# Linear attention with a gated FFN on one Trainium2 core: the readout of the attention state on 32x32 tiles, with q moving

## What is computed

```python
xn = _layernorm(x, axis=-1)
q = jax.nn.elu(split_heads(xn @ Wq.T)) + 1.0
k = jax.nn.elu(split_heads(xn @ Wk.T)) + 1.0
v = split_heads(xn @ Wv.T)
kv_state = jnp.einsum('bhnd,bhne->bhde', k, v)
k_state = k.sum(axis=2)
attn_out = jnp.einsum('bhnd,bhde->bhne', q, kv_state)
denom = jnp.maximum(jnp.einsum('bhnd,bhd->bhn', q, k_state), 1e-06)[..., None]
attn_out = (attn_out / denom).transpose(0, 2, 1, 3).reshape(b, s, d)
local = xp[:, :-2, :] * conv_w[:, 0] + xp[:, 1:-1, :] * conv_w[:, 1] + xp[:, 2:, :] * conv_w[:, 2] + conv_b
attn = (attn_out + local) @ Wp.T + bp
ffn = (silu(xn @ wg.T) * (xn @ wu.T)) @ wd.T      # wg, wu, wd: int32 weights / 127, hidden size 768
out = x + attn + ffn
```

## Time and profile before

| what | us |
|---|---|
| median of 3 runs | 505.0 (504.65 to 505.31) |
| the profiled execution | 504.68 |
| its span, first to last instruction | 503.0 |
| TensorE busy in the span | 490.9 (98%) |
| VectorE busy | 429.3 (85%) |
| ScalarE busy | 332.9 (66%) |
| GpSimd busy | 145.8 (29%) |

### The profile page before, as it was taken

The page is one execution under the profiler, slowest core; times in us unless marked ns, Lnnn a source line. Parts: engine busy times, 40 slices in busy tenths (PEclk is TensorE's granted clock), DMA queues, the critical chain, the costliest instruction groups (busy, mean ns, idle before and its releaser), DMA issues.

```text
span 503.0 us, 11007 instructions
## 1 busy us (share of the span) xinstructions
PE 490.9 (98%) x3957; PEld 305.2 (61%) x3957; DVE 429.3 (85%) x827; ACT 332.9 (66%) x522; POOL 145.8 (29%) x162
## 2 busy tenths in 40 slices
PE   7989998999999999999999999999999999999997
PEld 6545364755657475574756657475565747657576
DVE  6797998889888888888889888889988889897787
ACT  1878857667485666748577585767748567674771
POOL 4476034140501414032140502314041141401050
PEclk9999999999999999999999999999999999999999
DMA  8637332343335324252342325233342432234012
GB/s 300 192 46 166 64 106 42 86 111 56 130 44 142 69 47 132 44 155 42 100 108 42 125 42 167 42 83 106 53 133 42 129 79 42 86 50 76 3 42 85
DMA packets 68669, 45.36 MB, mean 90 GB/s; under 512 B 33440, under 2 KB 68128, under 8 KB 68640
## 3 DMA queue, kind: packets, MB, share of 16 engines
q1 hardware_dynamic: 59232, 35.66, 25.5%
q0 software_dynamic: 8448, 8.39, 11.1%
q10 hardware_dynamic: 960, 0.92, 0.5%
HBM read 20.32 MB, written 8.39 MB: 57 GB/s over the span
## 4 chain that ended last, share of the span: by engine, by line
PE 86%; DVE 8%; ACT 3%; issue 2%; POOL 0%; DVEq 0%; POOLq 0%; ACTq 0%
PE ps L1126 16%; PE ps L1285 15%; PE ps L1304 15%; PE ps L1294 14%; PE ps L1228 14%; PE ps L1184 5%; PE ps L1193 3%; PE ps L1247 2%; DVE hid L975 1%; DVE hl L981 1%; PE ps L1134 1%; DVE local L904 1%; PE ps L1169 1%; ACT hh L590 1%; DVE p_wl L745 1%
## 5 line engine op out<-in xcount | busy, mean ns | idle before, releaser
L582 ACT ACTIVATE act_g<-ps,scales 128x512 f32<-128x512 f32 x96 | 66.0, 687 | 42.0 <-PE ps L1294 40.0
L975 DVE SCALAR_TENSOR_TENSOR hid<-act_g,scales,ps 128x512 f32<-128x512 f32 x96 | 71.4, 744 | 21.3 <-ACT act_g L582 20.7
L981 DVE TENSOR_TENSOR hl<-hid,hh 128x512 f16<-128x512 f32 x96 | 66.7, 694 | 2.2 <-ACT hh L590 0.8
L365 POOL TENSOR_TENSOR xT<-xh,xl 128x1024 f32<-128x1024 f16 x15 | 31.8, 2122 | 112.5 <-issue 98.1
L590 ACT ACTIVATE hh<-hid 128x512 f16<-128x512 f32 x96 | 59.7, 622 | 5.4 <-DVE hid L975 5.4
L1285 PE MATMUL ps<-xh,g_wh 128*128 128x512 f16 x192 | 57.6, 382 | 2.1 <-DVE q_relu L930 1.2
L1294 PE MATMUL ps<-xl,g_wh 128*128 128x512 f16 x192 | 57.1, 379 | 0.0
L1294 PE MATMUL ps<-xl,u_wh 128*128 128x512 f16 x192 | 57.1, 379 | 0.0
L1285 PE MATMUL ps<-xh,u_wh 128*128 128x512 f16 x192 | 57.1, 379 | 0.0
L1304 PE MATMUL ps<-d_wh,hh 128*128 128x256 f16 x384 | 52.5, 273 | 1.3 <-DVE hid L975 1.3
L330 POOL TENSOR_SCALAR xn<-x_in,neg_mean,rstd 128x256 f32<-128x256 f32 x62 | 52.3, 857 | 4.3 <-POOL rstd L337 4.2
(11 more groups left out here) (162 smaller groups left out, 964.7 us busy)
## 6 DMA issues: line engine op xcount, KB each, us to landing
xb<-bp_sb SPq DMA_DIRECT2D x16, 512.0 KB, 3.3
xb<-in_L_attn_x_dram POOLq DMA_DIRECT2D x16, 512.0 KB, 5.9
x_in<-in_L_attn_x_dram SPq DMA_DIRECT2D x15, 512.0 KB, 4.2
out_dram<-out_sb SPq DMA_DIRECT2D x14, 512.0 KB, 2.9
wg_int<-in_L_ffn_w_gate_dram SPq DMA_DIRECT2D x1, 768.0 KB, 6.9
wu_int<-in_L_ffn_w_up_dram SPq DMA_DIRECT2D x1, 768.0 KB, 8.4
wd_int<-in_L_ffn_w_down_dram SPq DMA_DIRECT2D x1, 768.0 KB, 11.2
out_dram<-out_sb SPq DMA_DIRECT2D x3, 256.0 KB, 2.1
```

Of the source, the lines that this page charges most:

```text
L582: nc.scalar.activation(act_g[:, j % 2, :], ps[:, gate_bank(j), :], ACT.Silu, scale=silu_in).then_inc(silu_ready, 1)
L975: nc.vector.scalar_tensor_tensor(out=hid[:, j % 2, :], in0=act_g[:, j % 2, :], scalar=h_mul, in1=ps[:, gate_bank(j) + 1, :], op0=ALU.mult, ...
L981: nc.vector.tensor_tensor(hl[:, j, :], hid[:, j % 2, :], hh[:, j, :], ALU.subtract).then_inc(hl_ready, 1)
```

## The change

The readout is done the other way round. The state stays **stationary** in its compact form and q moves, so the result has channels on its partitions at once and there is nothing to turn back.

- `denominators`: four matmuls per chunk, `key_sums` (128 x 32, of which 8 columns are not zero) stationary on the four 32-column strips, 256 tokens of q moving. One half of the channels and one half of the tokens for each strip.
- `divide_one`: maximum and reciprocal of the 128 x 256 denominators, once per chunk. Of the 128 rows 32 hold denominators.
- `spread_den`: four DMAs on SyncE's queue copy each of the 8 rows to the 16 partitions of its head, 128 x 256 fp32 (128 KB) each, to `over_den` in q's layout.
- `divide_q`: q is multiplied by it, 128 x 1024.
- `numerators`: eight matmuls per chunk, each with a 32x32 block of the compact state stationary and 512 tokens of q moving. Those of the first half of the channels stand on the diagonal of the array (row strip r, column strip r) and write bank 4 (6 or 2 in the last step), those of the second half on row strip r, column strip r-1, and write the next bank.
- For that, wq's second half is loaded turned by 32 channels (three DMAs in place of one), and the accumulation of the second half stands on strips turned by one.
- `state` needs no spreading; the mask is reduced once to 128 x 32. `normalise` and `transpose_attn` are gone.
- `put_y` moves behind `hidden_low(0)`, `put_q` behind `hidden_low(4)`. `accumulate(1)` moves behind `gate_up(0)`, the numerators behind `gate_up(1)`. The last step is put in a new order.

Between `den_inv` and `q_divided` now lie the four DMAs; the numerators wait for `q_divided`. On SyncE `spread_den` stands first in the step, ahead of the load of x.

The diff, cut to its core:

```diff
+            def spread_den(b, c):
+                sp.wait_ge(den_inv, at(b, c, 1, 1))
+                for k in range(KT):
+                    for h in range(2):
+                        rows = slice((2 * k + h) * GROUP, (2 * k + h) * GROUP + HPB)
+                        sp.dma_start(over_den[:, c, k, h * DEN_TOKENS:(h + 1) * DEN_TOKENS],
+                                     rden[rows, c, :].unsqueeze(1).broadcast_to([HPB, HD, DEN_TOKENS])
+                                     ).then_inc(den_spread[c], 16)
...
             def step(b, c, attend, ahead):
+                if attend:
+                    spread_den(b - 1, c)
...
-            def normalise(b, c, p, banks):
...
+            def divide_one(b, c, bank):
+                dve.wait_ge(den_done, at(b, c, 1, 1))
...
+                nc.vector.tensor_scalar(den[:, :], ps[:, bank, 0:DEN_TOKENS], 1e-6, None, ALU.max).then_inc(den_kept, 1)
...
+                nc.vector.reciprocal(rden[:, c, :], den[:, :]).then_inc(den_inv, 1)
+
+            def divide_q(b, c):
+                dve.wait_ge(den_spread[c], b * 64 + 64)
+                nc.vector.tensor_tensor(q_sb[:, c, :, :], q_sb[:, c, :, :], over_den[:, c, :, :],
+                                        ALU.mult).then_inc(q_divided, 1)
...
                 if attend:
-                    normalise(b - 1, c, 0, QKV)
-                    normalise(b - 1, c, 1, QKV)
+                    divide_one(b - 1, c, DEN)
                     put_k(0)
...
                     relu_q()
-                    put_y(b - 1, c, 0, TURNED)
-                    put_y(b - 1, c, 1, TURNED)
+                    divide_q(b - 1, c)
...
+                        if j == 1 and attend:
+                            put_y(b - 1, c, 0, NUM)
+                            put_y(b - 1, c, 1, NUM)
+                        if j == 5 and attend:
+                            put_q(b, c)
...
+            def denominators(b, c, bank):
...
+                        ins = nc.tensor.matmul(ps[g:g + GROUP, bank, 0:DEN_TOKENS], key_sums[:, side_of(b), k, :],
+                                               q_sb[:, c, k, h * DEN_TOKENS:(h + 1) * DEN_TOKENS], start=True, stop=True,
+                                               tile_position=(0, g))
+                ins.then_inc(den_done, 1)
+
+            def numerators(b, c, banks):
+                pe.wait_ge(q_divided, at(b, c, 1, 1))
+                pe.sem_inc(num_due, 1)
+                for k in range(KT):
+                    for r in range(G):
+                        rows, g = slice(r * GROUP, (r + 1) * GROUP), (r - k) % G * GROUP
+                        ins = nc.tensor.matmul(ps[g:g + GROUP, banks[k], :], state[rows, side_of(b), k, :], q_sb[rows, c, k, :],
+                                               start=True, stop=True, tile_position=(r * GROUP, g))
+                ins.then_inc(num_done, 1)
...
-                    query(b - 1, c, 0, QKV)
-                    query(b - 1, c, 1, QKV)
+                    denominators(b - 1, c, DEN)
                 project_kv(1)
                 project_q()
                 accumulate(0)
+                gate_up(0)
+                accumulate(1)
+                gate_up(1)
                 if attend:
-                    transpose_attn(b - 1, c, 0, TURNED)
-                    transpose_attn(b - 1, c, 1, TURNED)
-                accumulate(1)
-                gate_up(0)
-                gate_up(1)
+                    numerators(b - 1, c, NUM)
```

More of the change, by code:

```diff
@@ L59, in at, with side_of @@
         return b * (CB * per_step) + (c * per_step + k)
+    def side_of(b):
+        return 1 if isinstance(b, int) and b == NB - 1 else 0
     with ExitStack() as ctx:
@@ L158, in build @@
         STATE = 6
[L159 to L160 removed]
+        DEN = 7
+        NUM = [4, 5]
         MAX_BANK = [7, STATE, 7]
@@ L294, in step @@
             def step(b, c, attend, ahead):
+                if attend:
+                    spread_den(b - 1, c)
+                if not ahead:
+                    spread_den(b, 0)
+                    spread_den(b, 1)
                 if not (isinstance(b, int) and b == NB - 1):
@@ L626, in step @@
                         hidden_high(j - 1)
-                    if attend and j == (Y_SPLIT[0] if ahead else 0):
+                    if attend and j == Y_SPLIT[0]:
                         y_high(b - 1, c, 0)
-                    if attend and j == (Y_SPLIT[1] if ahead else 1):
+                    if attend and j == Y_SPLIT[1]:
                         y_high(b - 1, c, 1)
@@ L1051, in step @@
                         hidden(j)
-                        if j == 0 and attend:
-                            put_q(b, c)
-                        elif j == 0:
+                        if j == 0 and not attend:
                             put_first_q()
@@ L1403, in step @@
                 else:
-                    first, second = 0, 1
                     gate_up(2)
+                    denominators(b, 0, LAST_DEN[0])
+                    gate_up(3)
+                    denominators(b, 1, LAST_DEN[1])
+                    gate_up(4)
                     project_y(b - 1, c, 0, WP)
-                    gate_up(3)
+                    gate_up(5)
                     project_y(b - 1, c, 1, WP)
-                    gate_up(4)
-                    pe.wait_ge(out_ready, at(b - 1, c, 2, 2))
-                    query(b, first, 0, LAST_QKV[0])
-                    query(b, first, 1, LAST_QKV[0])
-                    gate_up(5)
-                    pe.wait_ge(hid_ready, at(b, c, J, J - 1))
-                    query(b, second, 0, LAST_QKV[1])
-                    transpose_attn(b, first, 0, LAST_YT[0])
-                    pe.wait_ge(hid_ready, at(b, c, J, J))
-                    query(b, second, 1, LAST_QKV[1])
-                    transpose_attn(b, first, 1, LAST_YT[0])
-                    down(0, LAST_DOWN)
-                    project_y(b, first, 0, LAST_WP[0])
-                    project_y(b, first, 1, LAST_WP[0])
-                    transpose_attn(b, second, 0, LAST_YT[1])
-                    transpose_attn(b, second, 1, LAST_YT[1])
+                    numerators(b, 0, LAST_NUM[0])
+                    pe.wait_ge(hid_ready, at(b, c, J, J))
+                    pe.wait_ge(out_ready, at(b - 1, c, 2, 1))
+                    down(0, LAST_DOWN)
+                    numerators(b, 1, LAST_NUM[1])
+                    project_y(b, 0, 0, LAST_WP[0])
+                    project_y(b, 0, 1, LAST_WP[0])
+                    pe.wait_ge(out_ready, at(b - 1, c, 2, 2))
                     down(1, LAST_DOWN)
-                    project_y(b, second, 0, LAST_WP[1])
-                    project_y(b, second, 1, LAST_WP[1])
+                    project_y(b, 1, 0, LAST_WP[1])
+                    project_y(b, 1, 1, LAST_WP[1])
             is_wide = {}
```

136 lines of the change are left out of this document (62 added, 74 removed).

## The result

| | before | after |
|---|---|---|
| median of the runs, us | 505.0 (504.65 to 505.31) | 678.7 (676.96 to 680.07) |
| profiled execution, span, us | 503.0 | 678.5 |
| ratio of the medians | 1 | 1.344 [1.340, 1.348] |

The account below looks back on a forecast made before the run. TensorE, busy 98% of the span, was taken as the bound. Profiled 504.68 - 7.4 (13 steps) + 0.9 + 0.2 (start) + 1.5 (last step) = 499.9, median 0.3 above: 500.2 us; range 495 to 512.

Parts of the forecast that it names:

- the four DMAs: Spread of the denominators between reciprocal and divide_q: lands in 3.3 us, with 4.3 available and 0.7 more on TensorE, so hidden.
- a late spread: Rival: few partitions read 16 times take 5.9 us, numerators 0.9 late, kernel 512 us; chance 0.08.
- point of decision: In the late-spread rival: the spread's time decides the result from 5.0 us on.
- The chain up to it: Loop step from kv projection T: reciprocal ends T+6.8, q projected T+8.5, relu_q ends T+11.1, numerators start T+13.0.
- TensorE's sums: Per full step: -1.85 query, -0.93 transposes, +0.71 denominators, +1.14 numerators, +0.36 wait, together -0.57 us; 13 steps give -7.4.
- the last hl: Last hidden_low before the down projection, now behind put_q: done at 4.02, needed at 3.71, TensorE waits 0.36 us with the semaphore.
- The start: Before the loop: two more wq issues +0.9 us, mask reduction and a memset +0.2, neither hidden.
- The first readout step: First loop step with a readout: no term of its own, counted at -0.57 us like the other full steps.
- The last step: Final step, which reads out two chunks more: bounds -2.9 and +3.8 us, taken as +1.5.

Follow-up runs that it names:

- e1: The changed kernel without the four spread DMAs, q multiplied by a constant tile (division missing from the output): 508.5 us, ratio 1.006.
- e3: The changed kernel with the four DMAs reading a constant 128-row tile, each row once (division missing from the output): 508.1 us.
- e2: The changed kernel with each head's denominators on four rows, so 32 side-by-side rows are read 4 times each: 512.4 us.
- e4: The changed kernel with the eight denominator rows of a strip four partitions apart, each still read 16 times: 518.3 us.
- e5: e1 with GpSimd waiting for the state of the last two chunks before it adds xT of the next one: 502.6 us, ratio 0.995 against e1.

## Why the prediction was wrong, step by step

- **The step that failed is "the four DMAs"**: "512 KB as in the bias fill, which lands after 3.3 [...] I take 3.3: hidden." The bias fill reads and writes 128 partitions; these read from eight. Bytes and issue count were carried over, the source was not. Measured 14.8, and 170 us of the result (e1). With every row read once the same four land after 4.0 (e3: an issue is 0.5 to 0.6, not 0.45, and a landing 2.1, not 1.7); that would have been hidden, so the price of issues was not what failed. The rival *a late spread* named the mechanism, reading a few partitions many times, but took its price from another DMA that landed late, 5.9. That was no bound: no row of the trace before showed a read from few partitions, so the far end of that cost was open, and the range ended at 512 without it. It wanted a rival of its own with a price left open.
- **Its point of decision was right.** "It decides from 5.0 us on": at 4.6 (e2) TensorE waits only in three places for `divide_q`, one of them the 5.5 of the last step that e1 has too, at 5.1 (e4) in 13.
- **The chain up to it was right.** In e1 with T = 161.51 the reciprocal ends at T+6.8, q is projected at T+8.6, `relu_q` ends at T+11.1, the numerators start at T+13.0; forecast 6.8, 8.5, 11.1, 13.0.
- **TensorE's sums were right in sign and near in size.** Numerators 1.02 (forecast 1.14), denominators 0.57 (0.71), reciprocal 1.76 (1.74), `divide_q` 1.22. TensorE waits for the last hl 13 times, 0.2 at most, not 0.36. In e5, without DMA and without the collision, the 12 full steps after the first readout take 8.9 us less than before, 0.74 each; forecast was 0.57 (from a step of 29.83; every second one before took 29.99).
- **The start was wrong by 1.1**, on the safe side: the last kv projection ahead of the readouts starts at 67.61 in e5 and at 67.69 before. The two more issues and the mask didn't show.
- **The first readout step** was forecast like the others and takes 2.1 more (33.65, was 31.52). There `put_q` of the first chunk stands ahead of `relu_q`, and the longer reciprocal pushes it on: TensorE waits 2.8 for `relu_q` (3.1 in e1); before it waited 0.69 there and 0.74 for `hidden`.
- **The last step** was put at +1.5 out of bounds of -2.9 to +3.8, and is +5.2 (50.3, was 45.1). The prediction doesn't say what makes up the +3.8; the two reciprocals' 1.9 are half of it. What it lacked was that TensorE, once it stands for 5.5, comes back at half clock (1.96 for numerators that take 1.02), and that an hl beside GpSimd's taps there takes 1.65 in place of 0.68. What each of the two costs in the end isn't shown.
- **GpSimd's collision** was in no rival. It is 5.9 us (e1 against e5). Nothing was said of the masked product that the change makes smaller, though its place in time decides.

Together, by spans, for e5: 503.0 - 8.9 + 2.1 + 5.2 - 0.1 = 501.3; the span of its profiled execution is 501.4. In the changed kernel itself the 12 steps have grown by 143, the first readout step by 10.4 and the last stretch by 21.9.

## What to carry to other kernels

Price a DMA by the partitions that it reads from, not by its bytes alone: four transfers that replicate a few neighbouring rows took 14.8 us where the same four from 128 partitions take 4.0, and setting the same rows four partitions apart gave back 160 of the 170 us at no cost. Where the trace has no row of the kind, leave the far end open, and measure the transfer first. An instruction that takes ten times its usual length is read beside the other engine's timeline: a single wait that let the short one go first was worth 1.2%.

## What the runs showed of the hardware

- DMAs that read 8 neighbouring partitions: 512 KB in 14.8 us from the reciprocal's end, 47 GB/s while they are alone; the same rows two apart 94 GB/s and 8.8 us, four apart 182 GB/s and 5.1 us. SyncE's issues behind them took up to 2.8 us in place of 0.6.
- VectorE's product of two SBUF inputs, 64 columns: 0.22 us alone, or when it starts 0.02 ahead of GpSimd's sum of some 2.12; 2.13 when it starts 0.07 behind. Two `output`, with one input in PSUM, take 1.40 beside that sum as without it.
- Sixteen records of 512 columns on eight 32x32 tiles, four row strips writing each bank, each in its own 32 partitions: 1.02 us at full clock. The rule of the Trainium skill that different row tiles cannot access one PSUM bank at the same time (TensorEngine Tiling (Array Packing), Restrictions and Gotchas) doesn't hold for this form; by it they would have taken an estimated 3.5 (four times 0.87).
- A reciprocal of 256 columns takes 1.75 us, 4 columns take 0.18: 6.2 ns a column, as 4 and 32 columns in the kernel before had it.
